# Reordering the GpSimd weight work of the first token pair: the up unit's low half and the next tile's sums before the down weights' low halves

## The reference

```python
xn = _layernorm(x, axis=-1)
# attention: shift by one token, mix, three projections, the wkv recurrence
r = jnp.einsum('btc,hc->bth', xr, Wr); k = ...; v = ...
wkv = wkv_v4(k, v, wkv_w, wkv_u)
att = jnp.einsum('bth,ch->btc', jax.nn.sigmoid(r) * wkv, Wo)
# feed-forward
up_gate = jnp.einsum('bsd,hd->bsh', x, W1)
up_lin = jnp.einsum('bsd,hd->bsh', x, W3)
hidden = fwht(jax.nn.silu(up_gate) * up_lin)
out = jnp.einsum('bsh,dh->bsd', hidden, W2)
x = x + att + out
```

## Time and profile before

| | |
|---|---|
| Median of three runs | 2718.04 us |
| Profiled execution, its time | 2717.67 us |
| Its span, first to last instruction | 2715.9 us |
| TensorE busy | 2661.2 us (98%) |
| VectorE (DVE) busy | 2172.8 us (80%) |
| ScalarE (ACT) busy | 1331.0 us (49%) |
| GpSimd (POOL) busy | 239.0 us (9%) |
| DMA | 691.50 MB, mean 255 GB/s |
| Mean granted TensorE clock | 0.997 of full |

### The profile page before, as it was taken

How to read it: one execution, slowest core, us unless ns; L and a number is a source line. 1 busy time by engine, 2 the same in 40 slices (tenths; PEclk the granted TensorE clock), 3 DMA queues, 4 the chain that set the end, 5 groups by cost and what they waited for, 6 DMA issues and landing times.

```text
span 2715.9 us, 33856 instructions
## 1 busy us (share of the span) xinstructions
PE 2661.2 (98%) x11616; PEld 2181.4 (80%) x11616; DVE 2172.8 (80%) x2930; ACT 1331.0 (49%) x2125; POOL 239.0 (9%) x180
## 2 busy tenths in 40 slices
PE   7899999999999999999999999999999999999998
PEld 5677778888888888888888888888888888888887
DVE  7788878888868888688887888868888788877774
ACT  6666555444545345444464445644455444544442
POOL 3298900000000000000000000000000000000000
PEclk9999999999999999999999999999999999999999
DMA  6787777777868778687786867768687776876677
GB/s 247 272 317 267 260 263 248 268 254 234 278 226 281 241 248 279 223 266 251 247 281 235 273 227 268 262 245 271 217 278 251 258 258 231 271 240 223 229 229 267
DMA packets 244951, 691.50 MB, mean 255 GB/s; under 512 B 31920, under 2 KB 31920, under 8 KB 244272
## 3 DMA queue, kind: packets, MB, share of 16 engines
q1 hardware_dynamic: 244784, 689.34, 75.1%
HBM read 575.94 MB, written 113.30 MB: 254 GB/s over the span
## 4 chain that ended last, share of the span: by engine, by line
PE 88%; DVE 4%; POOL 3%; ACT 2%; issue 1%; DMA 1%; SPq 0%; ACTq 0%; DVEq 0%
PE gamma L870 12%; PE gamma L872 12%; PE gamma L873 12%; PE acc L880 10%; PE acc L882 10%; PE acc L881 10%; PE gamma L952 4%; PE gamma L954 4%; PE gamma L953 4%; PE alpha L870 2%; PE alpha L872 2%; PE alpha L873 2%; PE alpha L954 1%; PE alpha L952 1%; PE alpha L953 1%
## 5 line engine op out<-in xcount | busy, mean ns | idle before, releaser
L1066 ACT ACTIVATE step<-gamma 128x512 f32<-128x512 f32 x512 | 305.7, 597 | 827.0 <-PE gamma L873 811.7
L870 PE MATMUL gamma<-xs_high,wring 128*128 128x512 f32 x1280 | 500.0, 391 | 11.3 <-DVE step L1528 3.3
L872 PE MATMUL gamma<-xs_high,wring 128*128 128x512 f32 x1280 | 499.0, 390 | 0.0
L873 PE MATMUL gamma<-xs_low,wring 128*128 128x512 f32 x1280 | 499.0, 390 | 0.0
L880 PE MATMUL acc<-vring,hid 128*128 128x512 f32 x1232 | 481.4, 391 | 12.9 <-DVE res L1637 6.6
L882 PE MATMUL acc<-vring,hid 128*128 128x512 f32 x1232 | 479.9, 390 | 0.0
L881 PE MATMUL acc<-vring,hid 128*128 128x512 f32 x1232 | 479.9, 390 | 0.0
L870 PEld LDWEIGHTS gamma<-xs_high,wring 128*128 128x128 f32 x1280 | 240.8, 188 | 64.7 <-issue 10.6
L880 PEld LDWEIGHTS acc<-vring,hid 128*128 128x128 f32 x1232 | 231.6, 188 | 67.0 <-issue 10.2
L873 PEld LDWEIGHTS gamma<-xs_low,wring 128*128 128x128 f32 x1280 | 240.8, 188 | 50.4
L872 PEld LDWEIGHTS gamma<-xs_high,wring 128*128 128x128 f32 x1280 | 240.9, 188 | 49.6
(11 more groups left out here) (178 smaller groups left out, 4748.7 us busy)
## 6 DMA issues: line engine op xcount, KB each, us to landing
wring<-u_split SPq DMA_DIRECT2D x336, 512.0 KB, 4.1
vring<-d_split SPq DMA_DIRECT2D x288, 512.0 KB, 4.2
wring<-r_split SPq DMA_DIRECT2D x168, 512.0 KB, 4.2
raw<-spilled SPq DMA_DIRECT2D x160, 256.0 KB, 4.2
spilled<-step SPq DMA_DIRECT2D x128, 256.0 KB, 4.3
wlast<-u_split SPq DMA_DIRECT2D x112, 256.0 KB, 3.0
u_split<-wring SPq DMA_DIRECT2D x48, 512.0 KB, 4.0
res<-x SPq DMA_DIRECT2D x16, 1024.0 KB, 7.8
```

The lines of the kernel that those rows point to most:

```text
L870: pe.matmul(bank[:, :], w[:, 0, col], high, start=fresh and kt == 0, stop=False, skip_group_check=True)
L872: pe.matmul(bank[:, :], w[:, 1, col], high, start=False, stop=False, skip_group_check=True)
L873: last = pe.matmul(bank[:, :], w[:, 0, col], low, start=False, stop=kt == 1, skip_group_check=True)
L1066: act.activation(to, bank[:, :], ACT.Copy).then_inc(u_copied, 1)
```

## The change

On POOL, in step j, the low half of unit 3 of tile j and the four sums of tile j + 1 are formed first, and then the low halves of the down units of step j, and then as before those of units 0 to 2 of tile j + 1. A second table, `LOW_MADE_AT`, has the new order; everything that counts `split_lo` goes by it. SP stores in the new order of POOL: it now does `first_half`, the store of unit 3 and `store_hidden_b` before the stores of the down units. ScalarE's order and the table of `split_hi` stay. No instruction is added or taken away.

```diff
+def first_lows():
+
+    order = SPLITS[:15]
+    for j in range(FT + 1):
+        if j < FT:
+            order.append(("u", j, 3))
+        order += [("d", i) for i in down_splits(j)]
+        if j + 1 < FT:
+            order += [("u", j + 1, i) for i in range(3)]
+    return order
+
+
+LOW_MADE_AT = {u: n for n, u in enumerate(first_lows())}
@@ freed_by
-    return SPLIT_AT[("u", raw[1], 0) if raw[0] == "w1" else ("u", raw[1], 3) if raw[0] == "w3" else raw]
+    return LOW_MADE_AT[("u", raw[1], 0) if raw[0] == "w1" else ("u", raw[1], 3) if raw[0] == "w3" else raw]
@@ store_split
-                n = SPLIT_AT[unit]
+                n = LOW_MADE_AT[unit]
@@ first_up_step (SP)
-                for i in down_splits(j):
-                    store_split(("d", i))
                 first_half(0, j)
                 store_split(("u", j, 3))
                 if j:
                     store_hidden_b(0, j - 1)
+                for i in down_splits(j):
+                    store_split(("d", i))
@@ make_sums (POOL)
-                    pool.wait_ge(split_lo, SPLIT_AT["u", j - 1, 2] + 1)
+                    pool.wait_ge(split_lo, LOW_MADE_AT["u", j - 1, 2] + 1)
@@ POOL's steps
             for j in range(FT):
-                for i in down_splits(j):
-                    lo(("d", i))
                 lo(("u", j, 3))
                 if j + 1 < FT:
                     make_sums(j + 1)
+                for i in down_splits(j):
+                    lo(("d", i))
+                if j + 1 < FT:
                     for i in range(3):
                         lo(("u", j + 1, i))
@@ wait_split (TensorE)
-                pe.wait_ge(split_lo, SPLIT_AT[unit] + 1)
+                pe.wait_ge(split_lo, LOW_MADE_AT[unit] + 1)
```

## The result

The changed kernel takes 2740.74 us (median of four runs, 2738.11 to 2745.16) beside 2717.73 us for the kernel before: a ratio of 1.0082, 95% interval 1.007 to 1.0094. It is slower by some 23 us. The profiled execution has a span of 2739.9 us, 24.0 us more than before.

What follows compares the result with a forecast made beforehand. TensorE was taken to bound the kernel, busy 2661.2 of 2715.9 us. The terms 15.5 + 4.5 - 1.7 - 1.0 = +17.3 us, added to the median of 2718.04 us, gave 2735.3 us, range 2728 to 2744 us.

Steps and rivals of the forecast that it cites:

- Part 1: Steps 6, 9 and 11: down unit's low half comes behind unit 3 and the sums, TensorE waits longer; +15.5 us (12.8 to 19.6).
- Part 2: TensorE's clock behind the three new waits: each costs a clock fall, 3 x 1.5 = +4.5 us (4.2 to 5).
- Part 3: Sums end about 1.3 us earlier in steps with one down unit, shortening ScalarE's waits; net -1.7 us (-2.3 to 0).
- Part 5: VectorE's lateness, the 3.29 us wait at 240.71 us: POOL's sums no longer collide with what follows; -1.0 us (0 to -4.7).
- Part 4: Units 5, 9 and 12, SP's stores and raw loads stay covered, unit 12 in step 10 tightest; 0, at most +1 us.
- rival (a): VectorE catches up in TensorE's waits, its 3.29 us wait goes, sums run at 2.93 us; +10 to +12 us, chance 0.17.
- Behind the up phase: Steps from 350 us on should be the same, only shifted.
- Rival (b): Slow pace everywhere (sums 5.08 us as step 6 showed) and unit 12 late; +24 us, 2742 us, chance 0.13.

## Why the prediction was right, and where its sum was off

The way, the main mechanism and the places were as predicted: 2740.74 us lies between 2728 and 2744 us, and the loss of 23.0 us compares with 17.3 us forecast. That it lies within the range is in part luck: Parts 1 to 3 were all too small, and Part 5, for a reason that its text denied, gave back more than forecast. By the steps of the prediction, with the shifts of the table as measured:

**Part 1 (15.5 us forecast, 18.4 us measured).** Right in its mechanism, shown from both sides by the kernel with the three steps alone and the one without them, and by the kernel that moves TensorE's use. The waits were 8.25, 7.41 and 7.17 us where 6.9, 6.8 and 6.2 us were worked out. Three terms make up the difference. In step 6 POOL began unit 3 at 211.71 us, 1.59 us after TensorE had ended piece 2 (218.37 - 8.25 = 210.12 us), where 210.0 - 209.28 = 0.7 us were taken: ScalarE came late out of its exponentials, because it had waited 1.35 us for VectorE's z at 204.48 us. The kernel with the old order in the three steps has its wait of step 6 longer too, by 0.8 us, so this piece comes from the new order in the steps ahead. The low half of the down unit was put at 1.3 us. The two low halves of the step took 3.41 us in place of 2.52 us, held up by VectorE's scan. The four sums were put at 4.0 us and took 3.66 us in step 6 (212.39 to 216.05 us). In step 11 I took 3.4 us for them because a VectorE reciprocal lay there before. The two engines stood otherwise to each other by then, other VectorE instructions lay beside the sums, and they took 304.81 - 300.48 = 4.33 us:

```profile
300.48 1.17 POOL L779 TENSOR_TENSOR sums<-res 128x256 f32<-128x256 f32 x1
...
304.81 2.49 POOL L766 TENSOR_TENSOR vring<-raw,vring 128x512 fp32r<-128x512 f32 x2
```

POOL's pace went with what VectorE ran beside it: 0.72 us without a VectorE instruction beside it and 1.21 us with one for like sums, and a pair of low halves of 2.49 us without VectorE's product and scan and 3.41 us with them. Beside a reciprocal the sums kept the quick pace (0.74 to 0.76 us each in step 4 of the kernel before, 3.34 us the reciprocal). I had reckoned with the slower pace for the sums and not for the low half behind them.

**Part 2 (4.5 us forecast, 7.8 us measured).** The step holds and the kernel with the filled wait shows it as a price of its own, but the term was mis-sized. The 1.5 us is an estimate from the one fall in the earlier trace rows, 7 matmuls in 2.9 us in place of the 13 of the mean rate (1.4 us), rounded up. No run shows it for the new waits: behind them the low clock lasted 5 to 6 us, not 2.9 us, and cost 2.4, 2.6 and 2.8 us.

**Part 3 (-1.7 us forecast, about +0.4 us measured).** It failed in steps 0 to 5, which lost 1.6 us. The sums did come earlier: ScalarE stands for them 0.6 us, once, in place of 10.5 us in eight. But at 151.27 us it now waits 1.56 us for VectorE's z:

```profile
151.27 1.06 ACT L1129 ACTIVATE e<-z 128x1024 f32<-128x1024 f32 x1 [1.56 <-DVE z L1484]
```

The two VectorE instructions that make z took 1.78 us each there, and 1.23 and 1.22 us before. By the timelines POOL's larger low halves now lay beside them in place of the sums; no run isolates this. What was late next was VectorE. TensorE stood 2.29 us at 157.23 us in place of 1.56 us. In this trace a clock fall of 1.6 us stands behind it, and it delays TensorE so much that a wait of 0.78 us for POOL at 179 us goes. In the repeat of the changed kernel, and in the kernel with the old order in three steps, the same 2.29 us left the clock at 1.00, and steps 0 to 5 lost 1.5 us all the same. The gain in steps 13 to 15 did come, 1.2 us. In the two kernels with the thirteen steps alone no gain is left in the time.

**Part 4 (0).** Right. Unit 12 in step 10 has no wait in the changed kernel, nor have SP's stores or raw loads shown one; POOL's single wait for no cause that the profile shows is 0.16 us. The 0.4 us that Part 4 worked out for unit 12 do show where the long wait of step 9 is missing: with the old order in the three steps TensorE waits 0.30 us for it at 279.86 us. This fits the reason that was given for 0.

**Part 5 (-1.0 us forecast, -3.8 us measured).** The direction was right and its reason was not. Part 5 said that the new wait lets VectorE do only what it had done by 215.73 us, and took its gain from spared collisions. VectorE's wait went from 3.29 to 0.83 us, and with it the clock fall of 1.3 us (1.00 between 248.3 and 251.0 us). The kernel with step 6 alone shows that the new order there does it. The kernel with the scan moved shows what it rests on: with a product and the scan taken out of TensorE's wait, VectorE's wait is 3.02 us again. So the work that Part 5 counted for nothing is the gain, because TensorE stands still while it is done. In this half rival (a), VectorE catching up, was right.

**Behind the up phase (0 forecast, +2.0 us).** About 1.1 us is the clock fall of the down phase, which lasted longer (0.50 between 395 and 400 us and 0.91 between 400 and 405 us). The rest lies mostly in short waits for loads of down units, 2.3 us in four against 0.8 us in one. In the repeat this stretch is only +0.8 us in all, with 2.9 us in five such waits. It was not followed up, and no run tells what of it belongs to the change.

The errors of Parts 1, 2, 3 and of the last (+2.9, +3.3, +2.1, +2.0 us), of Part 5 (-2.8 us) and what lies ahead of the change (-0.8 us) add up to the 6.7 us between forecast and span. Had Part 5 been as small as forecast, the time would have come to about 2743.5 us, at the very edge of the range. Two small slips of the working change nothing: 210.63 - 210.47 is 0.16 us, not 0.14, and the upper bound of step 6 is 6.6 us, not 6.7. Rival (b), with the slow pace of 5.08 us for the sums, was near in time (2742 us) but for another reason: the sums were quicker than that, and the clock and the last low half were dearer.

## What to carry to other kernels

Before an engine's queue is reordered, mark for each product in it the moment at which its consumer asks for it: an order that is free in thirteen steps of sixteen loses most of 23 us (17.6 us by themselves) in the three where the consumer already stood waiting 1.3 to 1.7 us for the product. The pace of POOL's instructions went with VectorE's beside them (0.72 and 1.21 us for like sums, 2.49 and 3.41 us for a pair of low halves), so a pace must be read anew for the new place, for every instruction that lies in the wait. An idle TensorE can cost twice, for the wait and for the low clock behind it. The second part was 2.0 to 2.9 us behind waits of 7.2 to 8.3 us, and anything from nothing to 2.7 us behind waits of 2.1 to 3.3 us. And a long wait gives back what another engine can do in it.

## What was not expected of the hardware

The clock fall behind a wait of 7.2 to 8.3 us lasted about twice as long as that behind 3.3 us (5 to 6 us against 2.9 us). But the length of the wait doesn't set it alone: behind the waits of 2.84, 2.84 and 3.29 us of the kernel with the sums last, windows of 3.3, 4.1 and 5.8 us were at 0.55, 0.58 and 0.50. In the kernel with the wait filled by matmuls, idle times of 1.79, 1.14 and 0.93 us left the clock at 1.00. Nor does the same wait always bring a fall. The wait of 2.3 us in step 2 had 0.50 behind it in the changed kernel (159 to 161 us) and 1.00 in its repeat. That of 2.1 us in step 6 had 1.00 behind it with the old order in three steps, and 0.77 and then 0.50 in the kernel with both engines' new order (210.8 to 215 us). One of 3.25 us in the down phase had 1.00 behind it with the old order in three steps and 0.50 in the kernel before. What decides on a fall and sets its length stays open, and so a single trace here can differ from the next by such a fall, some 1.5 us.
